# Moving the small tiles of an attention, perceptron and non-local kernel behind its large ones

## What is computed

```python
def _L0_xattn_ref(...):                     # a decoder layer
    ln_out = layernorm(hidden_states, ln1_s, ln1_b)
    qkv = ln_out @ w_qkv + b_qkv
    q, k, v = jnp.split(qkv, 3, axis=-1)
    ctx = merge_heads(attention(split_heads(q), split_heads(k), split_heads(v), ltor_mask))
    x = hidden_states + (ctx @ w_ao + b_ao)
...
    q = ln_out @ w_q + b_q                  # ln_out = layernorm(x, ln2_s, ln2_b)
    kv = encoder_states @ w_kv + b_kv       # the same attention, 16 heads of 32
    x = x + (ctx @ w_co + b_co)
    ln_out = layernorm(x, ln3_s, ln3_b)
    return x + gelu(ln_out @ w1 + b1) @ w2 + b2
def _L1_xattn_ref(x, x_2, ...):             # a non-local block on its output
    W = jnp.einsum('bnc,bcm->bnm', theta_x, phi_x) / phi_x.shape[-1]
    y = jnp.einsum('bnm,bmc->bnc', W, g_x).transpose(0, 2, 1)
    return wy + x                           # wy: 1x1 convolution of y, batch-normed
```

## The kernel before

| tile | before | rest | after | rest |
|---|---|---|---|---|
| h_h, h_l, t_h, t_l, thx_h, m1_h, thw_h, p, pt, wst | 1152 and up | 0 | the same | 0 |
| w_h, w_l | 34432, 67200 | 0 | the same | 0 |
| x | 112768 | 0 | 112256 | 0 |
| xt_h, xt_l | 121184, 129376 | 32 | 120448, 128640 | 0 |
| e | 137568 | 32 | 136832 | 0 |
| et_h, et_l | 145760, 153952 | 32 | 145024, 153216 | 0 |
| q_h, q_l | 162144, 170336 | 32 | 161408, 169600 | 0 |
| k_h, k_l | 178528, 186720 | 32 | 177792, 185984 | 0 |
| v | 194912 | 32 | 194176 | 0 |
| ct_h, ct_l | 205856, 214048 | 32 | 204416, 212608 | 0 |
| res, ln_shift | 222240, 226336 | 32 | 220800, 224896 | 0 |

## Time and profile before

### The profile page before, as it was taken

One profiled execution on the slowest core, in us unless ns is written; L12 is line 12 of the kernel. 1 busy time (PEld: TensorE's weight loads), 2 busy tenths in 40 slices (PEclk: granted clock), 3 DMA queues, 4 the chain that ended last, 5 costly groups with the idle time before them and its releaser, 6 DMA issues. The chain is left out here.

```text
span 2119.7 us, 43342 instructions
## 1 busy us (share of the span) xinstructions
PE 2088.3 (99%) x14434; PEld 1658.0 (78%) x14434; DVE 1432.5 (68%) x3823; ACT 1172.0 (55%) x3270; POOL 421.4 (20%) x388
## 2 busy tenths in 40 slices
PE   8989999999999999999999998999999999999998
PEld 7867777777777777777777776788888888888887
DVE  7678887878889888888888889465344343435233
ACT  4377777877778877787777788421111111112111
POOL 1001111011013233122122211043031231313000
PEclk9989999999999999999999999999999999999999
DMA  8411211111123232222232222411101010101001
GB/s 278 145 30 53 64 60 50 56 64 46 54 75 109 84 110 64 81 84 70 68 94 63 75 94 80 137 63 44 43 22 45 20 45 30 39 35 45 22 23 45
DMA packets 126451, 143.78 MB, mean 68 GB/s; under 512 B 23888, under 2 KB 74192, under 8 KB 126288
## 3 DMA queue, kind: packets, MB, share of 16 engines
q1 hardware_dynamic: 126288, 141.80, 21.0%
HBM read 113.94 MB, written 27.79 MB: 67 GB/s over the span
## 5 line engine op out<-in xcount | busy, mean ns | idle before, releaser
L1119 ACT ACTIVATE A_p<-A_p,A_nmax 128x256 f32<-128x256 f32 x1024 | 509.2, 506 | 0.0
L1387 DVE TENSOR_TENSOR A_p<-A_sc,A_mk 128x1024 f32<-128x1024 f32 x256 | 312.2, 1219 | 151.1 <-PE A_tp L885 151.1
L1397 DVE CUSTOM_DVE_ANT_0 A_p<-A_p,A_ma 128x256 f32<-128x256 f32 x1024 | 385.6, 431 | 6.1 <-DVE A_p L1387 0.5
L1125 ACT ACTIVATE A_pt<-A_tp 128x512 f32<-128x512 f32 x512 | 277.4, 593 | 184.7 <-PE A_tp L885 184.5
L885 PEld LDWEIGHTS A_tp<-A_ident,A_p 128*128 128x128 f32 x2048 | 229.9, 141 | 73.0 <-issue 53.9
L885 PE MATMUL A_tp<-A_ident,A_p 128*128 128x128 f32 x2048 | 274.1, 277 | 1.4 <-ACT A_pt L1125 1.4
L1119 ACT ACTIVATION_READ_ACCUMULATOR A_p<-A_p,A_nmax 128x1 f32 x1024 | 202.0, 197 | 0.0
L1243 ACT ACTIVATE A_mk<-A_tp,A_cols 128x512 f32<-128x512 f32 x62 | 42.7, 689 | 276.6 <-PE A_tp L68 276.6
L1243 ACT ACTIVATE A_ma<-A_tp,A_cols 128x512 f32<-128x512 f32 x62 | 42.7, 688 | 247.3 <-PE A_tp L68 247.3
L672 POOL TENSOR_TENSOR A_res<-A_res,A_o_bias 128x512 f32<-128x512 f32 x64 | 82.7, 1315 | 407.6 <-DVE A_nmax L1397 259.7
L66 PE MATMUL A_banks<-A_xt_h,A_w_h 128*128 128x512 f32 x384 | 162.1, 422 | 1.0 <-DVE A_res L1366 0.5
(11 more groups left out here) (231 smaller groups left out, 4895.7 us busy)
## 6 DMA issues: line engine op xcount, KB each, us to landing
A_x<-x SPq DMA_DIRECT2D x96, 256.0 KB, 2.8
A_res<-x SPq DMA_DIRECT2D x64, 256.0 KB, 2.9
A_rt<-inverses SPq DMA_DIRECT2D x512, 32.0 KB, 1.8
x<-A_res SPq DMA_DIRECT2D x64, 256.0 KB, 2.1
A_e<-ctx SPq DMA_DIRECT2D x16, 512.0 KB, 4.0
inverses<-A_turned_inv SPq DMA_DIRECT2D x512, 1.0 KB
A_e<-ctx_t SPq DMA_DIRECT2D x16, 512.0 KB, 4.1
A_e<-L_xattn_w SPq DMA_DIRECT2D x32, 256.0 KB, 3.4
```

Source lines behind the costliest of these rows:

```text
L1119: act.activation(p[:, g % 2, j, t, :], p[:, g % 2, j, t, :], ACT.Exp, scale=-1.0, bias=nmax[:, g % 2, j, t:t + 1], accum_out=rsum[:, g % 2 ...
L1125: act.activation(pt[:, j, :, :], tp[:, j % 2, :].rearrange("p (c s) -> p c s", c=TPB), ACT.Copy)\
L1387: dve.tensor_tensor(p[:, g % 2, heads, :, :].rearrange("p j t s -> p j (t s)"), sc[:, heads, :], m, ALU.mult)\
L1397: dve.tensor_tensor_reduce(out=a_, in0=a_, in1=ma[:, b, t, :], scale=-1.0, scalar=BIG, op0=ALU.add, op1=ALU.min, accum_out=nmax[:, g % 2, ...
```

## The change

Sixteen small tiles (16 to 268 bytes in a partition) are allocated behind `ln_shift` and no longer between the large tiles. Nothing else is edited: on every engine the instructions, their order, their shapes and their waits are the same, and only the SBUF addresses differ. `rt` and `cx` stay between `v` and `ct_h`; they take 1024 bytes each.

```diff
@@ whole_network
         w_l = room.sb("w_l", [P, KT, 4 * H], F32R)
-        cols = room.sb("cols", [P, 10 * KT + 5 * OC + FT + 1])
-        lns_q = room.sb("lns_q", [P, 2, KT])
-        bias_sum = room.sb("bias_sum", [P, 2, 3, KT])
-        bias_q = room.sb("bias_q", [P, 2, KT])
         o_bias = room.sb("o_bias", [P, 2, H])
-        half = room.sb("half", [P, TT])
-        eps = room.sb("eps", [P, TT])
...
         x = room.sb("x", [P, TT, H])
-        stats = room.sb("stats", [P, TT, 6])
-        mv = room.sb("mv", [P, TT, 2])
-        ve = room.sb("ve", [P, TT])
-        rstd = room.sb("rstd", [P, TT])
-        nmean = room.sb("nmean", [P, TT])
         xt_h = room.sb("xt_h", [P, KT, TOK], F32R)
...
         v = room.sb("v", [P, TT, H])
-        nmax = room.sb("nmax", [P, 2, HPG, TPB])
-        rsum = room.sb("rsum", [P, 2, TPB, HPG])
-        rinv = room.sb("rinv", [P, 2, 32])
-        turned_inv = room.sb("turned_inv", [P, 2, 32])
         rt = room.sb("rt", [P, S])
-        shifted = room.sb("shifted", [P, 4, KT])
         cx = room.sb("cx", [P, S])
...
         ln_shift = room.sb("ln_shift", [P, H])
+        cols = room.sb("cols", [P, 10 * KT + 5 * OC + FT + 1])
+        lns_q = room.sb("lns_q", [P, 2, KT])
+        bias_sum = room.sb("bias_sum", [P, 2, 3, KT])
+        bias_q = room.sb("bias_q", [P, 2, KT])
+        half = room.sb("half", [P, TT])
+        eps = room.sb("eps", [P, TT])
+        stats = room.sb("stats", [P, TT, 6])
+        mv = room.sb("mv", [P, TT, 2])
+        ve = room.sb("ve", [P, TT])
+        rstd = room.sb("rstd", [P, TT])
+        nmean = room.sb("nmean", [P, TT])
+        nmax = room.sb("nmax", [P, 2, HPG, TPB])
+        rsum = room.sb("rsum", [P, 2, TPB, HPG])
+        rinv = room.sb("rinv", [P, 2, 32])
+        turned_inv = room.sb("turned_inv", [P, 2, 32])
+        shifted = room.sb("shifted", [P, 4, KT])
```

## The result

| | before | after |
|---|---|---|
| median of 4 runs | 2119.16 us (2117.84 to 2120.8) | 2091.93 us (2089.23 to 2092.84) |
| profiled execution, span | 2121.58 us, 2119.7 us | 2089.23 us, 2087.4 us |
| ratio, 95% interval | | 0.9869, 0.9852 to 0.9886 |

A forecast was written before the change was run, and what follows sets the result against it. TensorE's matmul rate was taken as the bound. The perceptron's 17.9 us plus attention's 11 make 29 us off the profiled 2121.6, giving 2091 us by the median; range 2084 to 2106 us.

The forecast's parts named there:

- The bound: Whole kernel: limited by the rate at which TensorE takes its matmuls; other engines keep slack and cost nothing on the path.
- The perceptron: Perceptron blocks: all 512-column matmuls settle near 226.8 ns, 94.3 us a block against 96.55, 17.9 us less in eight.
- Attention: Runs of 15 and 9 matmuls in 128 groups of heads: 0.086 us less a group, 11 us in all (6 to 15).
- The weighing: Attention's 2048 matmuls `banks<-pt,v`: taken as 0, with at most 3.4 us gained or as much lost.
- Element work and DMAs: ACT and DVE work and transfers: some 3 ns an instruction at most, covered by slack, so no cost on the path.
- like rests modulo 64: Matmuls of 512 columns: moved and weight tiles with equal address remainders modulo 64 bytes run at 226.8 ns, not 233.5.
- its slower rival: All large tiles alike modulo 512 might meet in one part of memory: 41 us slower, 2161 us; chance 0.04.
- the disturbances stay: Switches between tile pairs keep bringing uneven distances: perceptron gives 9.9 us, attention 6, so 2104 us; chance 0.12.
- it isn't the address: The fast 60 matmuls owe their speed to their place in the block; nothing moves, 2120 us; chance 0.10.
- attention gains nothing: Attention's short runs never settle or transposes wait for ACT; only the perceptron's 17.9 us are won, 2102 us; chance 0.06.

The follow-up runs named there:

- The pads of 64 and 128: Changed kernel with one pad of 64 or 128 bytes ahead of `xt_h`: 2107.53 us (ratio 0.9945) and 2117.34 us (0.9993).
- the tiles cut from `split`: Changed kernel with xt, et, q, k, ct cut out of one tile, offset 16 or 4 bytes: 2111.8 us (0.9963) and 2137.5 us (1.0083).

## Why the prediction was right, and where not

*The bound.* It was read rightly: TensorE's rate alone. No wait grew by more than 0.2 us, and the 32.7 us less of PE busy time are the 32.3 us less of span.

*The perceptron.* Predicted: 94.3 us in a block, measured 94.30. The level, taken as 226.8 ns from nine matmuls of before, measures 226.7 and holds for all but the matmuls behind transposes, and switches between tiles disturb nothing. Behind the last weighing of values the span is 17.7 us shorter, against 17.9 in the sum (its terms add up to 94.33 us, so it should have had 2.22 us a block and 17.8 in eight).

*Attention.* Predicted: 0.086 us in a group and 11 us in all. Measured: a body takes 76.97 us before and 76.19 after in the unrounded starts, 0.79 us less or 0.098 in a group, 12.6 us in 16 bodies. The parts came out otherwise than in the sum. The two runs shown in the earlier trace rows gained 0.04 and 0.08 us. Over all bodies the runs of 9 gained 0.02 us, where the sum had 0.02 to 0.04, since most of them are still disturbed behind their transposes (231, 236, 228, 232, 231 ns). The runs of 15 gained 0.084 us, where the sum had 0.03 to 0.08: behind their transposes nearly all of them stand at 227 ns from the second matmul on, which the perceptron's two samples didn't do. The term was under-sized by 1.6 us, within its bounds.

*The rest.* Read from the same matmuls in both traces, the span is shortened by 1.9 us up to the first weighing (at 123 us before), by 12.8 from there to the last weighing (at 1347 us) and by 17.7 behind it. The set-up was put at 0, and where its 1.9 us come from was not followed. In the middle stretch some 1.6 us come in between 124 and 146 us, as much as in two whole later bodies; between 120 and 140 us the mean granted clock was 0.83 in the trace of before and 0.92 in that of after. So this much is most likely the clock and not the addresses, and the rest of the stretch falls some 1 us short of 0.79 us a body. The weighing, whose bounds were +3.4 and -3.4 us, gave 0 as assumed: its 16 matmuls take 1.00 us in every layout. Element work and DMAs gave 0, as the near equal rows at 0 and 32 had said; after the change the ACT copy into `xt_h` is still at 596 ns.

```profile
L1092 ACT ACTIVATE A_xt_h<-A_tp 128x512 fp32r<-128x512 f32 x64 | 34.8, 596 | 5.1 <-PE A_tp L794 5.1
```

*The median.* Here the agreement is partly luck. The forecast was 29 us off the profiled execution, which lost 32.3, and 2091 us by the median, which is 2091.93 although the medians differ by only 27.2. Steady bodies and blocks alone give 12.6 + 18.0 = 30.6 us between the two traces. Only one execution of each kernel was profiled, so where the 3 us between 27.2 and 30.6 go isn't shown.

*The reason given for it.* Here the prediction was right by luck in one step. It said like rests modulo 64. Before the change the like pairs (`xt` past `et`, `w` past `h`) had rests that are also alike modulo 256, and no row had a pair that is alike modulo 64 and unlike modulo 256, so the rows couldn't tell. The pads of 64 and 128 could: had the change moved the tiles to multiples of 64 with other distances, it might have given 12 us or next to nothing, as they did. It gave 27 because all large tiles are multiples of 512 bytes long, and without small ones in between they keep one rest modulo 512. The prediction had noted that, but only as a danger (its slower rival); it is the thing that makes the gain.

*The rivals.* That the disturbances stay fell with the period of 94.30 us, that it isn't the address with the pad of 32 bytes, that attention gains nothing with its run of 15, and that all tiles at one rest modulo 512 collide with every row above. The Trainium skill, page "SBUF — State Buffer", section "Who interferes with whom", says that TensorE never waits on anyone at the SBUF and that its two read ports are independent. The runs disagree in effect: a pad of 32 bytes ahead of `xt_h` takes the stream from 226.7 to 233.3 ns a matmul, so the two reads do act on each other's time. Whether they do so at the ports isn't shown.

## What to carry to other kernels

When TensorE is busy all the time, measure the distance between starts of like matmuls, not their printed length, and compare groups that differ in their tiles alone; 20 ns over the time of the columns in one group and 13 in another is a finding. In streams like this one, of fp32r matmuls of 512 columns with a weight load for each, give the tiles of moving and stationary operands places that are alike modulo 256 bytes (put small tiles behind large ones, or pad). What counts is the operand being moved and the weights being loaded for the next matmul. Check the built addresses, since one odd tile of 32 bytes in between shifts everything behind it. Other types and shapes were not tried, apart from those named below. A round number in an address isn't the condition: a pad of 64 bytes between the two groups lost 16 of 27 us and one of 128 nearly all.

## What the runs showed of the hardware

In these runs the time of a stream of fp32r matmuls of 512 columns with a load of weights for each depends on the difference between the address that is moved and the one that is loaded, modulo 256 bytes: 226.7 ns at 0, 229 at +64, 233 to 234 at the others seen, 230 to 232 where the tiles cut from `split` begin at 16 bytes past a multiple of 32, and 237 where they begin at 4. Even at 0 there are 13 ns more than 512 columns at 2.4 GHz take. After a mismatched overlap the stream takes some seven matmuls to settle, behind transposes between one and ten. It goes through a fixed sequence (224, 231, 236, 228, 232 or 233, 231, 227) that it enters at different points: the kernel with `q` 32 bytes on goes through all of it on its way back from `sc<-q,h`, the changed kernel only through 232, 231 behind some of its transposes. Settled blocks repeat to within 1 ns in a trace (94.300 us, six times within 1 ns).

Not all matmuls behave so. In the set-up, products of 256 columns (`banks<-q,et`) ran no slower with unlike rests. Here is the kernel with `q` 32 bytes off `et`, and under it the changed kernel with both at one rest, from their timelines:

```profile
60.61 0.28 PE L66 MATMUL A_banks<-A_q_h,A_et_h 128*128 128x256 f32 x1
...
61.54 0.28 PE L68 MATMUL A_banks<-A_q_h,A_et_l 128*128 128x256 f32 x1
```

```profile
59.94 0.28 PE L66 MATMUL A_banks<-A_q_h,A_et_h 128*128 128x256 f32 x1
...
60.89 0.28 PE L68 MATMUL A_banks<-A_q_h,A_et_l 128*128 128x256 f32 x1
```

Eight distances take 0.93 us, 116 ns each, against 0.95 us, 119 ns each. There the unlike pair is the faster one by 2 to 3 ns, in the settled distances of the 29 runs of 12 as well (117 against 120 ns). Why the sign turns with the number of columns was not tried.
